# A fused feed-forward, attention, feed-forward block: part of the w3 weights split and turned by GpSimd, ScalarE and DMA instead of TensorE

## What is computed

```python
x = x + 0.5 * ffn(layernorm(x))          # one shared expert and 8 routed ones, the best 4 per row
x = x + attention(layernorm(x))          # 16 heads of 64, causal
x = x + 0.5 * ffn(layernorm(x))          # the same weights again

def swiglu(u, w1, w2, w3):               # 341 hidden units per expert
    h = einsum('...d,hd->...h', u, w1)
    v = einsum('...d,hd->...h', u, w2)
    return einsum('...h,dh->...d', sigmoid(h) * h * v, w3)
```

## Time and profile before

| | |
|---|---|
| median of 3 runs (lowest, highest) | 649.8 us (649.66, 649.97) |
| the profiled execution | 649.4 us |
| its span, first to last instruction | 647.7 us |
| busy: TensorE, VectorE, ScalarE, GpSimd | 634.1, 593.5, 562.2, 498.2 us |
| loads into the chip's memory | over by about 32 us |
| first pass without attention | up to about 97 us |

### The profile page before, as it was taken

How to read it: one execution, slowest core, us unless ns; L and a number is a source line. 1 busy time by engine, 2 the same in 40 slices (tenths; PEclk the granted TensorE clock), 3 DMA queues, 4 the chain that set the end, 5 groups by cost and what they waited for, 6 DMA issues and landing times.

```text
span 647.7 us, 21027 instructions
## 1 busy us (share of the span) xinstructions
PE 634.1 (98%) x7870; PEld 419.4 (65%) x7870; DVE 593.5 (92%) x1655; ACT 562.2 (87%) x1108; POOL 498.2 (77%) x617
## 2 busy tenths in 40 slices
PE   6799999999999999999999999999999999999997
PEld 5466665666676566667657666756666676666666
DVE  4998799999999999999999999999999998888887
ACT  5989997999999799999889999998999996566554
POOL 3254785899899779799968988986799997665545
PEclk9999999999999999999999999999999999999999
DMA  7900000487789278796746777973698874200000
GB/s 202 285 2 2 3 1 2 84 146 133 129 123 169 42 124 140 126 136 120 128 70 122 140 137 127 148 132 63 107 137 147 140 138 78 50 18 2 18 1 18
DMA packets 226489, 62.97 MB, mean 97 GB/s; under 512 B 213202, under 2 KB 225620, under 8 KB 226388
## 3 DMA queue, kind: packets, MB, share of 16 engines
q1 hardware_dynamic: 226388, 61.64, 53.4%
HBM read 7.87 MB, written 1.05 MB: 14 GB/s over the span
## 4 chain that ended last, share of the span: by engine, by line
PE 88%; DVE 6%; issue 2%; ACT 2%; DMA 0%; POOL 0%; SPq 0%; DVEq 0%; POOLq 0%; ACTq 0%
PE bank L1164 25%; PE bank L1166 24%; PE bank L1165 24%; PE bank L1344 8%; PE bank L1307 5%; DVE probs L1842 2%; DVE glu L1750 1%; DVE xs L1781 1%; PE bank L1172 1%; DVE glu L1755 1%; PE bank L1208 1%; DMA bias_b<-in_L_ffn_routing_bias 0%; ACT gluh L1511 0%; ACT glu L1487 0%; POOL glul L1127 0%
## 5 line engine op out<-in xcount | busy, mean ns | idle before, releaser
L1127 POOL TENSOR_TENSOR glul<-glu,gluh 128x512 f16<-128x512 f32 x191 | 218.9, 1162 | 78.4 <-ACT gluh L1511 77.9
L1131 POOL TENSOR_TENSOR paired<-probs,paired 128x512 f16<-128x512 f32 x160 | 184.2, 1163 | 22.5 <-ACT paired L1536 21.6
L1490 ACT ACTIVATE glu<-bank,tanh_scale 128x512 f32<-128x512 f32 x167 | 112.4, 680 | 37.9 <-PE bank L1166 34.4
L1528 ACT ACTIVATE probs<-probs,exp_bias 128x128 f32<-128x128 f32 (+3 forms) x256 | 129.1, 552 | 4.2 <-POOL exp_bias L1139 4.1
L1842 DVE CUSTOM_DVE_ANT_0 probs<-bank,causal,score_scale 128x128 f32<-128x128 f32 (+3 forms) x256 | 126.2, 545 | 3.6 <-POOL paired L1131 2.9
L1164 PE MATMUL bank<-w3h,gluh 128*128 128x128 f16 x708 | 125.3, 219 | 0.1
L1166 PE MATMUL bank<-w3h,glul 128*128 128x128 f16 x708 | 125.1, 219 | 0.0
L1165 PE MATMUL bank<-w3l,gluh 128*128 128x128 f16 x708 | 125.1, 219 | 0.0
L1750 DVE SCALAR_TENSOR_TENSOR glu<-glu,bank 128x512 f32<-128x512 f32 x167 | 113.5, 679 | 9.6 <-ACT glu L1490 9.0
L1511 ACT ACTIVATE gluh<-glu 128x512 f16<-128x512 f32 x191 | 113.4, 623 | 9.6 <-DVE glu L1755 8.8
L1755 DVE SCALAR_TENSOR_TENSOR glu<-glu,bank 128x512 f32<-128x512 f32 x167 | 114.7, 687 | 5.8
(11 more groups left out here) (247 smaller groups left out, 1613.4 us busy)
## 6 DMA issues: line engine op xcount, KB each, us to landing
pT<-paired SPq DMA_TRANSPOSE x160, 3.3
attention_raw<-in_L_attn_W_qkv SPq DMA_DIRECT2D x6, 256.0 KB, 5.2
xs<-in_L_attn_inputs SPq DMA_DIRECT2D x4, 256.0 KB, 4.1
vh<-in_L_ffn_W SPq DMA_DIRECT2D x6, 128.0 KB
pT<-in_L_ffn_W SPq DMA_DIRECT2D x6, 128.0 KB
out<-xs SPq DMA_DIRECT2D x3, 256.0 KB, 2.8
raw_more<-in_L_ffn_W SPq DMA_DIRECT2D x4, 128.0 KB
attention_raw<-in_L_attn_W_out SPq DMA_DIRECT2D x2, 256.0 KB, 6.2
```

The costliest lines, as they stand in the source:

```text
L1127: pool.tensor_tensor(glul[pair][:, :], g[:, :], gluh[pair][:, :], ALU.subtract).then_inc(glu_low)
L1131: pool.tensor_tensor(paired[n % PAIRED][:, 1, :], probs[n % PROBS][:, :], paired[n % PAIRED][:, 0, :], ALU.subtract).then_inc(probs_low)
L1490: act.activation(g[:, :], psum[b1.bank][:, :], ACT.Tanh, scale=tanh_scale[:, j:j + 1]).then_inc(tanh_made)
L1528: e = act.activation(pr[:, at:at + (qt + 1) * P], pr[:, at:at + (qt + 1) * P], ACT.Exp, bias=exp_bias[:, gp % 2, qt, head:head + 1], scale ...
```

## The change

- Experts 3 to 8 (`TURNED_W3 = 3`): w3 is no longer turned by TensorE. GpSimd scales the raw w3 in place (`scale_w3`), ScalarE copies the high part (`high_w3`) and GpSimd subtracts the low part (`low_w3`) into a staging buffer (the attention's `attn_pair`, unused at that time), high and low side by side for each tile; one DMA transpose (`turn_w3`) then puts both into w3. For that w3h and w3l become two halves of one buffer. `down` waits for the DMA instead of VectorE.
- `WARMING` goes from 12 to 7.
- Attention's weights: the scaling goes from ScalarE to GpSimd (`scale_attention_weight`).
- `ORDER` is a new table for all four engines.

```diff
-WARMING = 12
+WARMING = 7
...
+TURNED_W3 = 3
...
-        if len(turned) == 3:
+        if len(turned) == (3 if n < TURNED_W3 else 2):
...
-            if stage in "tuv":
+            if stage in "vr" and n >= TURNED_W3:
+                if stage == "v":
+                    self.spared[n] = self.free.popleft()
+                else:
+                    self.free.append(self.spared.pop(n))
+                    for kind in ("scale_w3", "high_w3", "low_w3", "turn_w3"):
+                        self.add(kind, n=n)
+                    self.weights_ready[n, 2] = TurnedW3(n)
...
+            self.add("scale_attention_weight", w=w)
             self.add("split_attention_weight", w=w)
...
     "tensor": (
-        "BFFFFFFFFFFFTTzFNTGTTSgNhhTGSTTTTThTddhhdhhGddShTTTddTdhhddTTdGhhShddTTTddTdhRhTdTXhhdzTdThhdTddghdh"
...
+        "FFFFFBFFTTzTTTGNSgNThhGSTTTTThTdhhdhdhGddSdTTThdhhTdddGhhShTTThddddddTRhhXddhzdTdThhgdhhhddhhddddhhhd"
...
-        w3h, w3l = sb("w3h", [P, len(PARTS), D], F16), sb("w3l", [P, len(PARTS), D], F16)
+        w3_pair = sb("w3", [P, len(PARTS), 2, D], F16)
+        w3h, w3l = w3_pair[:, :, 0, :], w3_pair[:, :, 1, :]
...
+        staged = lambda n: attn_pair[n % 2][:, :, :].rearrange("p a (j k) -> p (a j) k", k=D).rearrange("p (j a) k -> p j a k", a=2)[:, 0:len(TILES_OF[n])]
...
+                elif kind == "turn_w3":
+                    n = s["n"]
+                    q.wait_ge(w3_low, n - TURNED_W3 + 1)
+                    sp.dma_start_transpose(w3_pair[:, parts_of(n), :, :].rearrange("p j a d -> p (j a) d"),
+                                           staged(n).rearrange("p j a k -> p (j a k)")).then_inc(w3_turned[n % 2], 16)
...
+                elif kind == "scale_w3":
+                    n = s["n"]
+                    raw = raw3[n % RAWS][:, 0:len(TILES_OF[n]) * P]
+                    q.wait_ge(scales_made, group_of(n) + 1)
+                    pool.tensor_scalar(raw, raw, scale_of(n, 4), None, ALU.mult).then_inc(w3_scaled)
+                elif kind == "low_w3":
+                    n = s["n"]
+                    raw = raw3[n % RAWS][:, 0:len(TILES_OF[n]) * P].rearrange("p (j k) -> p j k", k=P)
+                    q.wait_ge(w3_high, n - TURNED_W3 + 1)
+                    pool.tensor_tensor(staged(n)[:, :, 1, :], raw, staged(n)[:, :, 0, :], ALU.subtract).then_inc(w3_low)
...
+                elif kind == "scale_attention_weight":
+                    w = s["w"]
+                    _, raw, _, _ = attention_weight(w)
+                    q.wait_ge(w_scaled, 1)
+                    pool.tensor_scalar(raw, raw, kind_of(w), None, ALU.mult).then_inc(weight_scaled)
...
+                    q.wait_ge(w3_low, NE - TURNED_W3)
                     pool.memset(vh[:, :, :, HEAD:SUMMED], 1.0).then_inc(sums_made)
...
+                if isinstance(use, TurnedW3):
+                    q.wait_ge(w3_turned[use.n % 2], 16 * ((use.n - TURNED_W3) // 2 + 1))
...
+                elif kind == "high_w3":
+                    n = s["n"]
+                    raw = raw3[n % RAWS][:, 0:len(TILES_OF[n]) * P].rearrange("p (j k) -> p j k", k=P)
+                    q.wait_ge(w3_scaled, n - TURNED_W3 + 1)
+                    if n >= TURNED_W3 + 2:
+                        q.wait_ge(w3_turned[n % 2], 16 * ((n - TURNED_W3) // 2))
+                    act.activation(staged(n)[:, :, 0, :], raw, ACT.Copy).then_inc(w3_high)
...
-                    q.wait_ge(w_scaled, 1)
-                    act.activation(raw, raw, ACT.Copy, scale=kind_of(w)).then_inc(weight_scaled)
                     q.wait_ge(weight_scaled, w + 1)
                     act.activation(high, raw, ACT.Copy).then_inc(weight_high)
```

More of the change, by code:

```diff
@@ L142 @@
 Turned = namedtuple("Turned", "n")
+TurnedW3 = namedtuple("TurnedW3", "n")
 class Schedule:
@@ L166, in __init__ @@
         self.added, self.measured, self.turned = {"A": 0, "V": 0}, {}, {}
[L167 removed]
+        self.weights_ready, self.spared = {}, {}
         self.native_ready, self.unscaled, self.scales_known = None, [], False
@@ L893, in macaron @@
         first_gathered, first_spread = signal("first_gathered"), signal("first_spread")
+        w3_scaled, w3_high, w3_low = signal("w3_scaled"), signal("w3_high"), signal("w3_low")
+        w3_turned = [signal(f"w3_turned{i}") for i in range(2)]
         eps_made = signal("eps_made")
@@ L1154, in drain_of @@
             def drain_of(use):
-                q.wait_ge(drained[use.bank], use.n + use.d)
+                if isinstance(use, TurnedW3):
+                    q.wait_ge(w3_turned[use.n % 2], 16 * ((use.n - TURNED_W3) // 2 + 1))
+                else:
+                    q.wait_ge(drained[use.bank], use.n + use.d)
             def x_there(ready):
@@ L1398, in scalar @@
                     else:
-                        high_of(split, psum[split.use.bank][:, 0:len(TILES_OF[n]) * D],
-                                w3h[:, parts_of(n), :].rearrange("p j d -> p (j d)"), scale_of(n, 4))
+                        high_of(split, by_part(psum[split.use.bank], n),
+                                w3h[:, parts_of(n), :], scale_of(n, 4))
+                elif kind == "high_w3":
[5 more added lines that the diff above has]
+                    act.activation(staged(n)[:, :, 0, :], raw, ACT.Copy).then_inc(w3_high)
                 elif kind == "measure" and s["by"] == "A":
@@ L1661, in vector @@
                     else:
-                        high, low = (w[:, parts_of(n), :].rearrange("p j d -> p (j d)") for w in (w3h, w3l))
-                        low_of(split, psum[split.use.bank][:, 0:len(TILES_OF[n]) * D], high, low, scale_of(n, 4))
+                        high, low = (w[:, parts_of(n), :] for w in (w3h, w3l))
+                        low_of(split, by_part(psum[split.use.bank], n), high, low, scale_of(n, 4))
                 elif kind == "norm_stats":
```

61 lines of the change are left out of this document (31 added, 30 removed), and 3 rows, old and new, of the table KINDS.

## The result

The changed kernel takes **652.5 us** in the median (652.47 to 652.65, 5 runs), beside 650.0 us (649.66 to 650.21, 5 runs) for the kernel before on the same chip: a ratio of 1.0044, 95% interval 1.0032 to 1.0055. The forecast was 646.7 us with a range of 645.0 to 649.0. The time is outside it, and the sign is wrong. The profiled execution took 652.47 us, with a span of 650.7 us; before, these were 649.4 and 647.7.

The account below looks back on a forecast made before the run. The prediction took TensorE as the bound, busy 634.1 of 647.7 us. From the profiled 649.4 us it took 1.9 for transposes and 1.2 for the start: 646.3, or 646.7 us as a median, range 645.0 to 649.0.

Parts of the forecast that it names:

- Transposes taken off TensorE: w3's transposes on TensorE fall from 30 to 10; 17 of them count, saving 1.9 us, bounds 1.9 and 2.2.
- The start: Up to the product at 26.09 us: fewer warming products and earlier transposes save 1.2 us, bounds 0 and 1.9.
- the first rival: At the start TensorE's clock rises later and the native pair takes some 3.8 us: 648.2 us, chance 0.14.
- The scalings' price: One GpSimd scaling of w3 or an attention weight was taken at 0.8 us, between 0.52 and 1.16.
- w3 on GpSimd: Experts 3 to 8: scaling, subtraction, copy and DMA transpose stay covered, price 0; 0.5 us if expert 5 lands longest.
- The attention's weights: Eight scalings move to GpSimd ahead of the first projection: price 0, range 0 to 1.2 us, once.
- Orders: Redrawn queues up to the end, with the third spread's 0.67 us stall: taken at 0, range -0.7 to +1.2 us.
- GpSimd is late once or twice: Rival: attention weights, expert 5 or a VectorE step slips, up to 0.95 us each; two give 648.5 us, chance 0.12.
- Slower in each head pair: Rival: in attention TensorE waits in each of 32 head pairs; at 0.2 us each 653.1 us, chance 0.06.

Follow-up runs that it names:

- e5: Changed kernel with all fourteen GpSimd scalings cut to half of their columns, same row of instructions: 645.8 us, ratio 0.9937.
- e6: Changed kernel with all fourteen GpSimd scalings cut to 8 columns: 646.0 us, ratio 0.9944.
- e2: Changed kernel with the router's exponential put ahead of the copy of the fifth attention weight in ScalarE's queue: 651.6 us, ratio 1.0031.
- e8: Changed kernel with twelve warming products instead of seven: 652.3 us, ratio 1.0033.
- e10: Changed kernel with only the attention's eight scalings on GpSimd cut to half of their columns: 648.0 us, ratio 0.9977.
- e11: Changed kernel with all fourteen GpSimd scalings written as a product of two tensors, nothing left out: 649.8 us, ratio 0.9997.
- e9: Changed kernel with only w3's six scalings on GpSimd cut to half of their columns: 649.6 us, ratio 1.0003.
- e1: Changed kernel with the scaling of the attention's eight weights back on ScalarE, orders otherwise as changed: 652.0 us, ratio 1.0035.
- e3: Kernel before with only the attention's eight scalings moved to GpSimd, placed by hand in the old orders: 657.0 us, ratio 1.0116.
- e4: Kernel before with only w3 of experts 3 to 8 turned by DMA, steps placed in the old orders: 658.3 us, ratio 1.0131.
- e14: Changed kernel with only w3's scalings of experts 4 and 5 as a product of two tensors: 654.9 us, ratio 1.0075.
- e12: Changed kernel with only the attention's eight scalings as a product of two tensors: 648.6 us, ratio 0.9980.

## Why the prediction was wrong, point by point

- **Transposes taken off TensorE: right.** The changed kernel has 10 w3 transposes, as forecast (rows below, of its groups by line), no wait of TensorE for a turned w3 in the changed kernel, and e5 and e6 at 645.8 and 646.0 us leave no room for a gain smaller than the 1.9 us plus the start's (0.8 us of e5's gain has no row). What was to follow from them didn't: the last product starts 3.1 us later, not 3 earlier, and the first projection at 105.39 us, not near 97.8 (it also stands behind more products now).

```profile
L1252 PE MATMUL bank<-ident,vl 128*128 128x128 f32 x7 | 1.1, 272 | 0.0
L1252 PE MATMUL bank<-ident,paired 128*128 128x128 f32 x3 | 0.5, 271 | 0.0
```

- **The start: right in kind, too large.** xn's transposes start at 8.22 us (about 8 was said), and the chain does meet expert 1's measure. But the pair lasts 2.83 us for 1.95, so the first spread comes at 14.26 rather than 13.2, the second at 22.96 rather than 22.4, and 0.7 us is kept of 1.2. This is the first rival's mechanism, the clock's rise, at half of its price. In e2, where the pair lasted 1.94 us and the spread came at 13.20, the first three-pass product still started at 18.69 us, since ScalarE was then late: the clock was not the only limit. The Trainium skill, TensorE: Matmul & The Clock Gate, The HAM clock gate, was cited for activity that releases the throttle. No row here speaks against it, but the number of early products doesn't decide: e8 with twelve warming products and e10 with seven both had the level up early (expert 0's transposes in 0.51 and 0.52 us) and lowered again ahead of the pair.
- **The scalings' price: the step that failed.** It is the term of "w3 on GpSimd" that both parts of the change use. "One operand read lies between: I take 0.8 and keep both ends." The bound from above was the subtraction's 1.16 us, on the argument that one operand less can't cost more. The scaling took 1.56 us. The form costs more than a product of two tensors (1.04, e11, where the second is the scale repeated); why it does, no run shows. 20.6 us of scalings went onto GpSimd (8 x 1.56, 4 x 1.25, 2 x 1.57) where I counted 10.4. Near the price that I took the forecast holds (e5: 645.8 for 646.7), with some luck in it: the start gave 0.5 us less than I took, and 0.8 us came from where I named nothing.
- **The attention's weights: price 0, range 0 to 1.2, once: the wait that was missed.** The prediction looked at the last reader, the first projection, found 0.3 us of slack, and put the risk there; it was 0.66 us late. The costly reader was another, which the text never named: ScalarE's copies. Each copy waits for its scaling with the rest of ScalarE's queue behind it, the router's exponential among it. The working priced what the moved step costs on its new engine and left out who waits for it in order on the old one. It cost 2.34 us there and 1.7 us of lower clock (with the 0.66 us, 4.7; e10 gave 4.5 us back).
- **Orders: 0.** The third spread's wait of 0.67 us did go. New ones of 0.88, 0.43, 0.28 and 0.21 us came between 40 and 60 us. In e5 and e9 all four are gone, so they came of w3's scalings, but one of 0.50 us for w1l takes their place; e6, with scalings of 0.31 us, keeps it (0.49), so that half a microsecond belongs to the orders.
- **The rivals.** "GpSimd is late once or twice" was the right one. It priced a slip at up to 0.95 us, from the length of one collision in the earlier trace rows. A slip of a queue is as long as the work that is queued ahead, here two subtractions and a scaling, 3.8 us from 77.91 to 81.72, and that wasn't in the sum. "Slower in each head pair" was the only rival on the slower side, and it did not occur (0.96 us idle from 112 to 600 us, for 0.90 before). The chance of 0.05 for slower came of having no rival in which the two terms priced at 0, w3's and the attention's, were wrong together.
- **The range** took in the bounds of a price that was bounded on one side by an argument, not by a row.

## What to carry to other kernels

When work moves to an engine, price its instruction from a row of the same form on that engine. Without such a row there is no upper bound, and a cover of some 5 us isn't enough for fourteen steps of unknown length: ask at which price the forecast breaks (here between 0.94 and 1.56 us). Then go through the queues of those who wait for the moved step, and name what stands behind each waiting instruction: the bill came at a reader that had nothing to do with the change. Undoing one edit in an order that was drawn around it, or putting it into an order that wasn't, prices the order, not the edit (e1, e3, e4); making the edit's instruction shorter in place does price it (e5, e9, e10).

## What the runs showed of the hardware

- GpSimd's product with a scalar for each partition takes 1.56 us for 128x512 in 32-bit floats, 0.94 for 256 columns (e5) and 0.31 for 8 (e6); the same product of two tensors, one of them repeated, takes 1.04 us (e11), and a subtraction with 16-bit output 1.16.
- VectorE's small steps on 32-bit data in SBUF (silu_scale, silu_back, spread) last until a two-tensor instruction of GpSimd ends: 1.86 us for 0.53 (e11, e14). Beside GpSimd's scalar form they took 0.53 and 0.75 us (e5, e12). Not every small step is held: a RECIPROCAL of 128x8 at 55.53 us of the changed kernel took 0.20 us beside a two-tensor instruction. The Trainium skill, GPSIMD Engine Reference, Specifications, names such contention for VectorE instructions in a 2-port mode or with two SBUF inputs; these rows agree on VectorE's side and add that GpSimd's form matters.
- TensorE's granted clock fell to the lower level around an idle time of 2.34 us in the changed kernel and of 2.35 us in e14, and did not after one of 2.34 us in e8, nor after 2.0 us in e9. It fell after 3.78 us in e4 and 4.41 us in e3. I expected no fall at all, from a pause of 0.56 us in the earlier trace rows. What decides between the cases of 2.34 us stays open.
- The time at which the clock rises at the start differs between profiles of kernels that are the same up to there (pair of 1.94 to 3.68 us); with the start of before it did not (1.95 or 1.96 us in four). The column of granted clock shows 1.00 from 0 to 16 us for ten of the twelve, at either pace (0.89 in e8, 0.79 in e10): there the spacing of like products is the witness, not the column.
